# Second normalisation of an RWKV layer: mean and variance once per token in 128 columns, spread by DMA, quarters every 24 steps

## The reference

```python
x = L0_attn_x
xn = _layernorm(x, axis=-1)
x = x + _L0_attn_ref(xn, ...) + _L0_ffn_ref(xn, ...)

# _L0_attn_ref, the RWKV layer
h = _layer_norm(x, ln1_g, ln1_b);  k, v = xk @ w_tk, xv @ w_tv;  r = sigmoid(xr @ w_tr)
y = _wkv(time_decay, time_first, k, v)        # a scan over the 1024 tokens
x = x + r * y
h2 = _layer_norm(x, ln2_g, ln2_b)             # the second normalisation: mean and variance over 128 channels
hp2 = _shift(h2)
ck = h2 * cmix_k + hp2 * (1.0 - cmix_k);  cr = h2 * cmix_r + hp2 * (1.0 - cmix_r)
kk = jnp.square(jax.nn.relu(ck @ w_ck))
x = x + sigmoid(cr @ w_cr) * (kk @ w_cv)

# _L0_ffn_ref: 16 heads of 8 channels, 2 batches
attn = softmax(q @ k.T);  ctx = attn @ v;  out = _svd_moe(ctx, o...)
```

## Time and profile before

| | |
|---|---|
| timed runs (3) | median 445.06 us, 442.83 to 445.18 |
| profiled execution | 443.83 us, of which 441.7 us span from its first to its last instruction |
| busy, share of the span | PE 96%, DVE 87%, ACT 77%, POOL 43% |
| chain that ended last | PE 87%, DVE 8%, ACT 3% |
| granted TensorE clock | full (2.4 GHz) in all of the 40 slices |

### The profile page before, as it was taken

How to read it: one execution, slowest core, us unless ns; L and a number is a source line. 1 busy time by engine, 2 the same in 40 slices (tenths; PEclk the granted TensorE clock), 3 DMA queues, 4 the chain that set the end, 5 groups by cost and what they waited for, 6 DMA issues and landing times.

```text
span 441.7 us, 8603 instructions
## 1 busy us (share of the span) xinstructions
PE 423.2 (96%) x3266; PEld 146.3 (33%) x3266; DVE 382.5 (87%) x657; ACT 341.7 (77%) x466; POOL 191.6 (43%) x271
## 2 busy tenths in 40 slices
PE   1999989999999999999999999999999999999997
PEld 1744222334233222233223322323333332332335
DVE  8469899998999998799999789999978998978182
ACT  3447837879887898788799869878986987898572
POOL 5039681935551625382352537506363620423200
PEclk9999999999999999999999999999999999999999
DMA  6004403141414151404242422333332322050311
GB/s 242 12 7 54 48 7 33 20 67 19 64 22 68 19 67 17 65 9 68 24 62 22 64 23 46 40 53 32 52 36 25 54 26 45 3 130 5 108 47 50
DMA packets 45797, 20.46 MB, mean 46 GB/s; under 512 B 36828, under 2 KB 37500, under 8 KB 45756
## 3 DMA queue, kind: packets, MB, share of 16 engines
q1 hardware_dynamic: 44630, 18.96, 27.7%
q10 hardware_dynamic: 1126, 0.95, 0.6%
HBM read 4.74 MB, written 4.98 MB: 22 GB/s over the span
## 4 chain that ended last, share of the span: by engine, by line
PE 87%; DVE 8%; ACT 3%; issue 1%; DMA 1%; DVEq 0%
PE banks L1498 27%; PE banks L1485 22%; PE banks L1388 18%; PE banks L1449 8%; DVE half_max L1198 5%; PE banks L1349 3%; ACT probs L985 2%; PE banks L1245 1%; PE banks L1428 1%; PE banks L1355 1%; PE banks L1284 1%; PE banks L1436 1%; PE banks L1341 1%; PE banks L1250 1%; DVE stats L1044 1%
## 5 line engine op out<-in xcount | busy, mean ns | idle before, releaser
L1198 DVE TENSOR_REDUCE half_max<-banks 128x1 f32<-128x512 f32 x512 | 318.4, 683 | 19.0 <-PE banks L1388 17.2
L985 ACT ACTIVATE probs<-banks 128x1024 f32<-128x1024 f32 x256 | 248.2, 1023 | 51.5 <-PE banks L1485 48.3
L1498 PE MATMUL banks<-probs,v_op 128*32 128x512 f32 x1024 | 136.4, 605 | 0.0
L1388 PE MATMUL banks<-k_main,q_main 64*128 64x512 bf16 x512 | 117.0, 384 | 5.1 <-DVE half_max L1198 3.3
L1485 PE MATMUL banks<-q_main,k_main 64*128 64x512 bf16 x512 | 99.3, 377 | 0.4 <-ACT probs L985 0.2
L1485 PE MATMUL banks<-q_tail,k_tail 35*128 35x512 bf16 x512 | 99.3, 377 | 0.0
L1388 PEld LDWEIGHTS banks<-k_main,q_main 64*128 64x128 bf16 x512 | 36.7, 93 | 150.2 <-DVE half_max L1198 131.9
L1485 PEld LDWEIGHTS banks<-q_tail,k_tail 35*128 35x128 bf16 x512 | 27.1, 94 | 26.2
L1485 PEld LDWEIGHTS banks<-q_main,k_main 64*128 64x128 bf16 x512 | 26.4, 95 | 25.1 <-ACT probs L985 10.2
L1498 PEld LDWEIGHTS banks<-probs,v_op 128*32 128x32 f32 x1024 | 20.1, 108 | 31.3 <-issue 30.3
L731 POOL TENSOR_TENSOR work<-work 128x512 f32<-128x512 f32 x16 | 16.7, 1041 | 28.6 <-ACT work L974 28.6
(11 more groups left out here) (186 smaller groups left out, 422.3 us busy)
## 6 DMA issues: line engine op xcount, KB each, us to landing
ctx_dram<-ctx_sb SPq DMA_DIRECT2D x15, 256.0 KB, 2.0
q_main<-parts SPq DMA_DIRECT2D x60, 48.0 KB
k_main<-parts SPq DMA_DIRECT2D x60, 48.0 KB
mat_sb<-in_mats_dram SPq DMA_DIRECT2D x2, 768.0 KB, 5.2
v_op<-V SPq DMA_DIRECT2D x16, 64.0 KB, 3.9
parts<-ctx_dram SPq DMA_DIRECT2D x4, 256.0 KB, 4.4
q_main<-parts SPq DMA_DIRECT2D x30, 32.0 KB
k_main<-parts SPq DMA_DIRECT2D x30, 32.0 KB
```

Of the source, the lines that this page charges most:

```text
L985: a.activation(probs[:, (2 * step + h) % 4, :, :], banks[:, 2 * h:2 * h + 2, :], ACT.Exp).then_inc(b_read, 1)
L1198: v.tensor_reduce(half_max[:, n % 2, u:u + 1], ring_bank(at), axis=AX.X, op=ALU.max).then_inc(a_read, 1)
L1388: mm(dst, q_main[HALF * e:HALF * (e + 1), s, P * c:P * c + P], k_main[HALF * e:HALF * (e + 1), s, CHUNK * h:CHUNK * h + CHUNK], start=True ...
L1498: last = mm(banks[g:g + 32, PV_BANK, :], v_op[:, s % 2, step, e, :], probs[:, (2 * step + h) % 4, e, :], start=(step == 0), stop=True, ski ...
```

## The change

- The mean and the variance are products of 128 columns instead of 512: group g of 32 output rows gets the sum over the channels for tokens 128 g to 128 g + 127 (`means_of`), so each token's mean stands in 32 rows of one group and not in all 128 rows.
- ACT copies the 128 columns to `row_stats` (at t = mean + 1, which frees the ring entry, `mean_kept`), issues a DMA that stores rows 0, 32, 64 and 96 to DRAM (4 x 128 numbers), and at mean + 2 waits for its landing and issues a load of these 512 numbers into all 128 rows (`wide_stats`). The variance goes the same way from var + 1: Ln (frees the entry), Exp, store; at var + 2 the load.
- DVE subtracts the mean from `wide_stats` at mean + 4 instead of from the bank at mean; POOL squares at var - 1 and scales by `wide_stats` at t = 36.
- The local steps behind move by five (var by four): var 32, cr 40, ck 41 to 44, cv 47. `GAP` falls from 26 to 24, so that the last quarter's cv stands at step 119 and not at 120.
- The windows are gone: all operations read and write the kept tensors in place (`quarter(t, q)`), and x1 has two buffers.

```diff
-GAP = 26
+GAP = 24
-PRODUCT_STEP = {"mean": 26, "var": 28, "cr": 35, "ck0": 36, "ck1": 37, "ck2": 38, "ck3": 39, "cv": 42}
+PRODUCT_STEP = {"mean": 26, "var": 32, "cr": 40, "ck0": 41, "ck1": 42, "ck2": 43, "ck3": 44, "cv": 47}
...
-            taken_by = {"mean": (centred2, q + 1), "var": (log_var_q, q + 1), "cr": (cr_step, 2 * q + 1),
+            taken_by = {"mean": (mean_kept, q + 1), "var": (log_var_q, q + 1), "cr": (cr_step, 2 * q + 1),
...
-                    for window, whole in ((k_q, k_of), (gate_q, gate_of), (v_q, v_of), (x_q, xnT[:, :, :])):
-                        g.tensor_copy(window[:, :, :], whole[:, :, bass.ds(q * QT, QT)]).then_inc(windows, 1)
...
+            def store_stats(i):
+                act.dma_start(stat_dram[i], row_stats[0:P:32, :]).then_inc(stat_out, 16)
+            def load_stats(i):
+                act.wait_ge(stat_out, 16 * (i + 1))
+                act.dma_start(wide_stats[:, :], bass.AP(stat_dram.tensor, i * CHUNK, [[0, P], [1, CHUNK]])
+                              ).then_inc(stat_in, 16)
...
-                if t == PRODUCT_STEP["var"]:
+                if t == PRODUCT_STEP["mean"] + 1:
+                    act.wait_ge(mean2_ps, q + 1)
+                    a.copy(row_stats[:, :], ring_bank(ring.index(("job", "mean", q)))[:, 0:P]).then_inc(mean_kept, 1)
+                    act.wait_ge(mean_kept, q + 1)
+                    store_stats(2 * q)
+                if t == PRODUCT_STEP["mean"] + 2:
+                    if q > 0:
+                        act.wait_ge(h2_hat, q)
+                    load_stats(2 * q)
+                if t == PRODUCT_STEP["var"] + 1:
                     act.wait_ge(var2_ps, q + 1)
-                    a.activation(flat(rs2), ring_bank(ring.index(("job", "var", q))), ACT.Ln, bias=eps_c[:, 0:1]
-                                 ).then_inc(log_var_q, 1)
-                if t == PRODUCT_STEP["var"] + 1:
+                    a.activation(row_stats[:, :], ring_bank(ring.index(("job", "var", q)))[:, 0:P], ACT.Ln,
+                                 bias=eps_c[:, 0:1]).then_inc(log_var_q, 1)
                     act.wait_ge(log_var_q, q + 1)
-                    a.activation(rs2[:, :, :], rs2[:, :, :], ACT.Exp, scale=-0.5).then_inc(rs2_ready, 1)
-                if t in (33, 34):
+                    a.activation(row_stats[:, :], row_stats[:, :], ACT.Exp, scale=-0.5).then_inc(rs2_rows, 1)
+                    act.wait_ge(rs2_rows, q + 1)
+                    store_stats(2 * q + 1)
+                if t == PRODUCT_STEP["var"] + 2:
+                    act.wait_ge(centred2, q + 1)
+                    load_stats(2 * q + 1)
+                if t in (38, 39):
...
-                if t == PRODUCT_STEP["mean"]:
-                    dve.wait_ge(mean2_ps, q + 1)
-                    v.tensor_tensor(flat(xc2), flat(x1), ring_bank(ring.index(("job", "mean", q))), ALU.subtract
-                                    ).then_inc(centred2, 1)
+                if t == PRODUCT_STEP["mean"] + 4:
+                    dve.wait_ge(stat_in, 32 * q + 16)
+                    v.tensor_tensor(flat(xc2), flat(x1[q % 2]), wide_stats[:, :], ALU.subtract).then_inc(centred2, 1)
...
+                def means_of(moving):
+                    for g in range(0, P, 32):
+                        last = mm(dst[g:g + 32, 0:P], mean_w[:, 0:32], moving[:, 4 * g:4 * g + P], start=True, stop=True)
+                    return last
```

More of the change, by code:

```diff
@@ L128, in build @@
         k_tail = sb("k_tail", [P, 2, T], BF16)
-        quarter_in = sb("quarter_in", [P, CHUNKS, CHUNK])
+        row_stats = sb("row_stats", [P, P])
+        wide_stats = sb("wide_stats", [P, CHUNK])
         v_op = sb("v_op", [P, 2, KEY_TILES, 2, 32])
@@ L193, in build @@
         carried = sem("carried")
-        windows = sem("windows")
+        mean_kept = sem("mean_kept")
+        rs2_rows = sem("rs2_rows")
+        stat_out = sem("stat_out")
+        stat_in = sem("stat_in")
         run_max_ready = sem("run_max_ready")
@@ L401, in out_bank, with quarter @@
             return bank(2) if (n, i) == (3, 1) else ring_bank(len(ring) + 2 * (n - 2) + i)
+        def quarter(t, q):
+            return t[:, :, QT * q:QT * (q + 1)]
         def quarters_at(step):
@@ L663, in branch @@
                     pool.wait_ge(run_max_ready, q * 2 + 2)
-                    pool.wait_ge(windows, q * 4 + 1)
+                    pool.wait_ge(carried, q + 1)
                     g.tensor_tensor(d1[:, :, :], before, after, ALU.subtract).then_inc(exponents, 1)
-                    g.tensor_tensor(d2[:, :, :], k_q[:, :, :], after, ALU.subtract).then_inc(exponents, 1)
+                    g.tensor_tensor(d2[:, :, :], quarter(k_of, q), after, ALU.subtract).then_inc(exponents, 1)
                 if t == 7:
-                    g.tensor_tensor(d3[:, :, :], before, k_q[:, :, :], ALU.subtract).then_inc(exponents, 1)
+                    g.tensor_tensor(d3[:, :, :], before, quarter(k_of, q), ALU.subtract).then_inc(exponents, 1)
                 if t == 13:
@@ L681, in branch @@
                     pool.wait_ge(weights_ready, q * 4 + 2)
-                    pool.wait_ge(windows, q * 4 + 4)
-                    g.tensor_tensor(ev[:, :, :], hi_u[:, :, :], v_q[:, :, :], ALU.mult).then_inc(ev_ready, 1)
+                    g.tensor_tensor(quarter(k_of, q), hi_u[:, :, :], quarter(v_of, q), ALU.mult).then_inc(ev_ready, 1)
                 if t == 18:
@@ L701, in branch @@
                     pool.wait_ge(ry_ready, q + 1)
-                    g.tensor_tensor(x1[:, :, :], num[:, :, :], x_q[:, :, :], ALU.add).then_inc(x1_ready, 1)
-                if t == PRODUCT_STEP["mean"] + 1:
+                    g.tensor_tensor(x1[q % 2][:, :, :], num[:, :, :], quarter(xnT, q), ALU.add).then_inc(x1_ready, 1)
+                if t == PRODUCT_STEP["var"] - 1:
                     pool.wait_ge(centred2, q + 1)
                     g.tensor_tensor(sq2[:, :, :], xc2[:, :, :], xc2[:, :, :], ALU.mult).then_inc(squared2, 1)
-                if t == 31:
+                if t == 36:
                     if q > 0:
@@ L738, in branch @@
                     for b in range(B):
-                        last = g.tensor_tensor(there[:, b, :, :], x1[:, b, :].rearrange("c (p k) -> c p k", k=CHUNK // P),
+                        last = g.tensor_tensor(there[:, b, :, :], x1[q % 2][:, b, :].rearrange("c (p k) -> c p k", k=CHUNK // P),
                                                gx[:, b, :].rearrange("c (p k) -> c p k", k=CHUNK // P), ALU.add)
@@ L1150, in branch @@
                     dve.wait_ge(carried, q + 1)
-                    dve.wait_ge(windows, q * 4 + 1)
-                    scan(t - 2, run_max, k_q, col("decay").to_broadcast([P, QT]), ALU.max, ALU.add, run_max_ready)
+                    scan(t - 2, run_max, quarter(k_of, q), col("decay").to_broadcast([P, QT]), ALU.max, ALU.add, run_max_ready)
                 if t in (9, 10):
@@ L1173, in normalise_ctx @@
                 if n == 0:
-                    dve.wait_ge(windows, QUARTERS * 4)
+                    dve.wait_ge(x1_ready, QUARTERS)
                     dve.wait_ge(v_ready, CHUNKS)
@@ L1461, in product @@
                     pe.wait_ge(x1_ready, q + 1)
-                    columns(mean_w, flat(x1)).then_inc(mean2_ps, 1)
+                    means_of(flat(x1[q % 2])).then_inc(mean2_ps, 1)
                 elif name == "var":
                     pe.wait_ge(squared2, q + 1)
-                    columns(mean_w, flat(sq2)).then_inc(var2_ps, 1)
+                    means_of(flat(sq2)).then_inc(var2_ps, 1)
                 elif name == "cr":
```

31 lines of the change are left out of this document (15 added, 16 removed).

## The result

| | before | after |
|---|---|---|
| timed runs | median 444.46 us (442.83 to 445.18, 4 runs) | median 469.82 us (468.96 to 470.78, 4 runs) |
| profiled execution | 443.83 us, span 441.7 | 469.91 us, span 468.2 |
| granted TensorE clock, mean | 1.000 | 0.982 |

The ratio of the medians is 1.058, with a 95% interval of 1.056 to 1.060: the change costs 25 us. The forecast was 465.2, with a range of 453 to 471.

The account below looks back on a forecast made before the run. PE's chain of 2.49 us a step bounds the kernel, with DVE at 2.48 having no room. Three quarters at 6.15 make 18.5, the last 2.9: 21.4 on the profiled 443.83 gives 465.2, range 453 to 471.

Parts of the forecast that it names:

- The holds: Third fill after each mean and var product waits for ACT's read behind its pair: 2.0 us each, eight holds, 16.1.
- DVE's work without cover: Local steps 26 to 36: scans and subtraction no longer beside products; with the holds, 6.85 us a quarter against 2.6 before.
- the subtraction: DVE's subtraction of the mean, at local step 30 without a product beside it: costs 0.67 us and covers var product's 0.22.
- ACT's meeting: Steps 39 to 42: ACT's work of two quarters 24 steps apart coincides, costing 1.95 us in each of three quarters.
- cr's read: Step 41: third fill waits for ACT's read of cr, last in step 40's list, losing 1.15 us.
- The pair's delay in steps 39 and 40: ACT's pair of exponentials runs late, so the second half of step 40's scores starts 0.4 us late.
- DVE has gained time in these stalls, so nothing: Step 40: the two scans of t = 16 cost nothing, with the cr product behind them.
- The fourth rival: After each hold, PE's standing still lowers the clock for a step: 18 us more, 483; chance 0.03.
- The end part: Last quarter's cv one step earlier only moves a product of the same length to another step: costs nothing.
- DMAs, windows: New stores and loads land before they are needed; the windows' copies leave POOL, off the path: both cost nothing.
- the third rival: Stores land late, 5 us against 2.3 at most, holding ACT: 4 us more, 469; chance 0.05.
- the last quarter: The quarter with no younger one beside it: 4.9 us against 2.0 before, a difference of 2.9.

Follow-up runs that it names:

- experiment 1: The changed kernel with ACT's copy of the mean and Ln of the variance in the product's own step, ahead of the next pair of exponentials: 449.90 us.
- experiment 2: The kernel before with one line changed, ACT taking Ln of the variance (512 columns) one step later, at var + 1: 455.92 us.
- experiment 5: The kernel of experiment 1 with ACT taking the older quarter's work first in each step: 452.05 us.
- experiment 6: The kernel of experiment 1 with POOL's second mixing addition held until DVE's two scans of the younger quarter are done: 448.77 us.
- experiment 7: The kernel of experiment 6 with ACT taking work from local step 40 on (reads of cr and ck) ahead of the younger quarter: 446.87 us.
- experiment 3: The changed kernel with eight zero-weight matmuls on PE before the third fill's wait in each of the eight holds: 463.07 us.
- experiment 4: The changed kernel with cv one local step later (48), so that the last stands in step 120 as before: 466.30 us.
- experiment 9: The kernel of experiment 1 with GAP back at 26 and mean, var and all behind them placed as in the kernel before: 442.84 us.
- experiment 8: The kernel before with only the windows removed, all operations using the kept tensors in place: 443.64 us.

## Why the prediction was right, and where its terms were off

**The holds.** The step that carried the forecast held: 2.0 per hold, third fill at 2.9. Measured where the clock stayed full: steps 51, 33 and 105 of 4.55, 4.65 and 4.65, third fill at 3.01, 3.10 and 3.10. The copy took 0.27 and the Ln 0.37, against the 0.30 with the hop to PE that I took and the estimate of 0.41. Experiments 1 and 2 show the cause from both sides, by taking it away from after and putting it into before.

**DVE's work without cover.** 6.85 was worked out for local steps 26 to 36. Taken from steps at full clock, the excess over a bare step is 0.25 (26), 2.06 (27), 0.52 (28), 0.50 (31), 0.25 (32), 2.16 (33), 0.52 (34) and 0.54 (35): 6.8. (The steps in which the maxima are turned, in after 29 and 37, have 2.66, as in before where nothing else stands in them.) Var's product was not covered by the subtraction (0.25 for 0), the subtraction cost 0.50 for 0.67, the two holds 4.22 for 4.0, and what stands behind the second 1.06 for 1.45; that the sum came out so near is luck, in that these errors cancelled.

**ACT's meeting.** 1.95 was forecast, in three steps (0.4, 1.15, 0.4). Measured 1.1: 0.10 in step 40, 1.01 in step 41 (4.36 for the 3.35 of a step with a product), nothing in 42. The 1.15 for cr's read was nearly right. The pair's delay in steps 39 and 40 was swallowed, which I had only as the lower bound. What I had not seen is that the scans would run beside POOL's addition and the first of them double; "DVE has gained time in these stalls, so nothing" was wrong as a statement of cost, though it shows in the time only once ACT's order is mended (experiments 5 to 7).

**The clock.** The fourth rival had 0.03 and a price of 18. It happened, at five of eight holds, and cost 5.0 (experiment 3). The forecast's 0.78 rested on a clock of 1.000 throughout, but in before PE never stood for 2 us within the steps, so that row could not speak for it. Nor is a full clock sure in before: of its 23 executions timed beside experiment 3 four had a mean of 0.996. The price was too high for another reason: of the eight holds three had no half clock behind them, and where it came, step 27 with the one behind it was longer by some 1.0 and not 2.3 (5.34 + 3.25 against 4.56 + 3.01). I had let the matmuls of a whole step double, but that stretch at half clock runs from 141.94 to 145.35, and half of it, 1.7, is the most that it can take from PE. The five cost 0.8 to 1.4 each; why not 1.7, and which hold is followed by half clock and which isn't, stays open. In two of the four timed runs of after the clock's mean was lower still (0.978 and 0.974 for 0.982), so five is no fixed number. The Trainium skill's warning of idle gaps, cited in the prediction, was right in kind: the clock fell here behind standstills of 1.75 and 1.85. The gaps that the section names are longer than these; the measurement decides.

**The end part.** That moving cv "from one step to another in the end part" costs nothing was wrong by 1.7 in these executions (0.6 to 1.4 in the others with cv at 119). I had asked what the step costs and not what stands behind cv in PE's list: at step 119 it is the values that finish a pair, with the context's DMAs to follow (experiment 4).

**DMAs, windows.** In after PE never waited for work that a store or a load had held up. ACT's issues took 0.50 to 0.55 for a store, above the 0.35 to 0.37 of the earlier trace rows, and 0.32 to 0.36 for a load; those of the stores lie in or right behind holds. The loads landed after 3.0 to 3.9, a little sooner than in the earlier trace rows. Of the stores the profile's views give no landing; the semaphore's updates in the trace put it at 1.6 to 1.9 for the mean and, for three of the four variances, at 3.4, well above the 2.3 that the third rival took as the most of the earlier trace rows. Behind these three ACT issued the loads 3.4 to 4.0 after the stores, so in after that rival was near and did not bite. In experiments 1 and 9, where the steps are shorter, it did, at some 1.0 and 1.5 us. All of these stores stand beside SP's loads of q and k; no run takes those away, so that they are the reason is not shown. Removing the windows cost and gave nothing (experiment 8).

**The sum.** 21.4 was forecast and 26.1 came in the profiled executions. Terms: the last quarter and local steps 26 to 36 as forecast, within 0.3 a quarter; ACT's meeting 2.6 less in three quarters; clock 5.0 more; end part 1.7 more; opening 0.4. From cv to cv it was 77.1 and 77.8 for the 77 forecast, but with half clock in both; with PE busy in the holds (experiment 3) it was 76.1. So the holds and DVE's work, the terms that carried the forecast, were right as mechanism and size, and the 4.6 that the total was off is the clock and the end part, which I had at nothing, less what I took too much for ACT.

## What to carry to other kernels

When a buffer of a ring changes its reader, compare the place of the new reader in its own engine's list with the time at which the buffer is due: one step too late costs a whole pair's length at each use, however short the read is (0.27 us of copy cost 2). When a long operation moves along a list, ask what stands behind it in the new place, above all the first link of a chain of DMAs. And where two corrections of one stretch each fail alone, look for a second engine that is late at the same place before giving up either. Last, a shorter step asks for its DMAs sooner: room that a stall gave is gone when the stall is (experiment 1).

## What the runs showed of the hardware

- PE stood for 1.75 or 1.85 us in a stream that was otherwise all but full, and the granted clock then fell to half in five of eight cases; with zero-weight matmuls in the same gap it stayed at 1.000 in all four runs. Each fall cost 0.8 to 1.4.
- A DVE scan with two operands from SBUF that began beside a running two-operand addition of POOL took 1.46 us for 0.74 (1.65 with a longer overlap, experiment 5), while POOL's kept its 1.2 (1.18 to 1.20).
- A DMA of 4 rows to DRAM occupied ACT's queue for 0.50 to 0.55 us; that of 256 KB into 128 rows for 0.32 to 0.36. The same 2 KB store landed after 1.6 us in one place and 3.4 to 3.7 in another, beside SP's loads of q and k; whether those are the reason was not tested.
